# Quantised FFN weights stored untransposed and read back by transposing DMAs, in place of 132 TensorE transposes

## The chip, the cores and the metric

One Trainium2 chip, one of its cores. The metric is the time of one execution on the device in microseconds (us), median over runs. The core has TensorE (PE, with a separate row PEld for its weight loads), VectorE (DVE), ScalarE (ACT), GpSimd (POOL) and SyncE (SP). In this kernel SP issues almost every DMA, and its queue is worked through in order.

## The reference, cut to what matters

The input is `x` of 8 x 512 rows of 512 numbers, with a context of 8 x 77 rows of 384. One layer is a cross attention (8 heads of 64) and a feed-forward block whose weights and activations are fake-quantised to 8 bit.

```python
def _act_fake_quant(x, clip_factor):
    scale = sigmoid(clip_factor) * max(abs(x)) / 127       # one scale for the whole tensor
    return clip(round(x / scale), -128, 127) * scale
def _weight_fake_quant(w):
    scale = max(abs(w), axis=1, keepdims=True) / 127       # one scale for each row
    return clip(round(w / scale), -128, 127) * scale

x = x + xattn(layernorm(x), ctx, Wq, Wk, Wv, Wo, bo)
xq = _act_fake_quant(layernorm(x), clip_x)
gate, up = xq @ wq(w_gate).T, xq @ wq(w_up).T              # w_gate, w_up: 1408 x 512
h = _act_fake_quant(silu(gate) * up, clip_down)
x = x + h @ wq(w_down).T                                   # w_down: 512 x 1408
```

The two activation scales are maxima over everything, so the block falls into three stages that can't overlap on TensorE: attention for all rows, gate and up for all rows, down for all rows. The weights are contracted over their last dimension, so TensorE needs them with that dimension on the partitions: transposed.

## The kernel before

Work is cut into 8 batches `b` of 512 rows and 32 tiles `n` of 128 rows. Every instruction of every engine is put into a queue in program order by `Chain.add` (L18) and `Chain.dma` (L34, whose issue is recorded as L37), with the semaphore waits written out by hand. An engine takes its queue in order, and so does SP.

The attention stage is the loop `attend(s)` over s = 0 to 31, with b = s // 4 and t = s % 4. Step s makes the scores of tile s+1 (`S`, `soft_*`), the probabilities' transposes of tile s (`PT`, L425), the output projection of tile s-5 (`wo`, L459 to 461), its residual sum `x1` (`residual`, L485) and its second norm `n2` for tile s-6 (`normed`, L509). `x1` and `n2` go to HBM (`x_rows`, `n_rows`) from rings of three buffers: `residual(n)` waits for the store of `x1` of tile n-3, `normed(n)` for the store of `n2` of tile n-3. The query product `q_chunk` for the batches ahead needs `xTs`, the input split in two parts by `split_hi` (ACT, L208) and `split_lo` (POOL and DVE, L212); those stand in steps t = 2 and t = 3, and the first `q_chunk(b + 2, 0)` (L846) at the end of step t = 3. At the end of step t = 0, after the last product of `PV(b - 1, 3)`, SP issues `load_vb(b)` (L357), twelve small DMAs, and `load_kb(b + 1)`.

Beside it the FFN weights are quantised, one row block `i` per step, 26 in all: 22 of gate and up (128 x 512) and 4 of down (128 x 1408, `big` below). Step s issues `w_load(s)` on SP (L681), takes the row maximum, scale and inverse of block s-1 on DVE (L552 to L561), rounds it on ACT (L568) and makes the integers `wint` on POOL (`w_integer`, L574). One step later `w_turn` (L588) transposes `wint` on TensorE, 4 times 128 x 128 for a small block and 11 times for a big one, `w_out` (L597) evicts PSUM to `wstg` on ACT, and SP stores it to the scratch `wgud` or `wdd` in runs of 128 numbers. The scratch is laid out as the later stages want it in SBUF.

At the end of step 31 SP loads the whole of `wgud` into `wgu` (2816 KB, L885) with a plain DMA. It waits for `gone`, the last readers of the SBUF that `wgu` takes over. After the loop come the last tiles: `wo(27)`, `normed(26)`, `residual(27)` (L891), the products `PV(7, 0)` to `PV(7, 3)`, whose ACT and DVE evictions stand behind those two in their queues, then `wo(28)` to `wo(31)`. The first FFN product waits for `wgu` and the quantised activations. `wd` (1408 KB, L949) is loaded after the first scale is known, and needed in the last stage.

Of the kernel before, what the change touches and what calls it, by code (L numbers as in the profile page):

```python
# [5 lines left out]
class Chain:  # L6
# [27 lines left out]
    def dma(self, engine, out, in_, waits, sig):  # L34
        f32, f32r = mybir.dt.float32, mybir.dt.float32r
        out, in_ = (v.bitcast(f32) if v.dtype == f32r else v for v in (out, in_))
        return self.add(engine, lambda e: e.dma_start(out, in_), waits, sig, 16)  # L37

    def run(self, engine, e):
        for need, fn, sem, by in self.queue[engine]:  # L40
# [14 lines left out]
def block_kernel(nc, x, xT, ctxT, Wq, Wk, Wv, Wo, bo, clip_x, clip_h, w_gate, w_up, w_down, out):  # L55
    f32, f32r, bf16 = mybir.dt.float32, mybir.dt.float32r, mybir.dt.bfloat16
    ALU, ACT, AX = mybir.AluOpType, mybir.ActivationFunctionType, mybir.AxisListType
    NB, L, H, D, I = 8, 77, 8, 512, 1408
    NT, NI = 32, 11
    HL = H * L  # L60
    MAGIC = 12582912.0
# [4 lines left out]
    with ctx:  # L66
        c = Chain(nc, ctx)
        add, dma = c.add, c.dma

        def sb(stack, name, shape, dt=f32):  # L70
            return stack.enter_context(nc.sbuf_tensor(name, shape, dt))

        def dram(name, shape, dt):
            return nc.dram_tensor(name, shape, dt, kind="Internal").ap()
# [2 lines left out]
        vd = dram("v_halves", (NB * L, 2, D), f32)  # L77
        x1d = dram("x1_rows", (NT, 128, D), f32)
        n2d = dram("n2_rows", (NT, 128, D), f32)
        wgud = dram("wgu_ints", (128, 4, 2 * I), bf16)  # L80
        wdd = dram("wd_ints", (128, NI, D), bf16)
        hd = dram("h_spill", (2, 128, NI * 512), f32)


# [65 lines left out]
        vbd = sb(late, "vbd", [128, 2, 8, 128], f32r)  # L150
        pts = sb(late, "pts", [128, 2, 5, 512], f32r)
        wraw = sb(late, "wraw", [128, 2, I])
        wint = sb(late, "wint", [128, I], bf16)
        wstg = sb(late, "wstg", [128, 2, NI, 128], bf16)
        late.close()
        early.close()

# [372 lines left out]
        wg_v = w_gate.rearrange("(r p) n -> r p n", p=128)  # L530
        wu_v = w_up.rearrange("(r p) n -> r p n", p=128)
        wd_v = w_down.rearrange("(r p) n -> r p n", p=128)
        t_wr, t_wy, t_wb, t_wt, t_we, t_ws, t_wiv = [Tokens() for _ in range(7)]
        t_we["last"] = None


        W_ORDER = [*range(22)]
# [3 lines left out]
        def w_row(i):  # L541
            i = W_ORDER[i]
            return (wg_v[i], 4) if i < 11 else (wu_v[i - 11], 4) if i < 22 else (wd_v[i - 22], NI)
# [27 lines left out]
        def w_integer(i):  # L571
            n = w_row(i)[1]
            v = wraw[:, i % 2, 0:n * 128]
            t_wb[i] = add("pool", lambda e: e.tensor_scalar(wint[:, 0:n * 128], v, -MAGIC, 1.0, ALU.add,  # L574
                                                            ALU.mult), [t_wy[i], t_wt.get(i - 1)], "w_int")

        MIb = MI[:, :].bitcast(bf16)

        PTb = PTP[:, :].bitcast(bf16)

        def w_turn(i, n):

            nb = w_row(i)[1]
            dst = [(MIb if k < 8 else PTb)[:, (k if k < 8 else k + 2) * 128:][:, 0:128] for k in range(nb)]

            def fn(e):
                for k in range(nb):
                    m = e.transpose(dst[k], wint[:, k * 128:k * 128 + 128], identB[:, :])  # L588
                return m
            t_wt[i] = add("pe", fn, [t_wb[i], t_idB, t_we.get("last")] + ([t_pl[n - 1]] if nb > 8 else []),  # L590
                          "w_tr")

        def w_out(i, n, part):
            nb = w_row(i)[1]
            src, k0, k1, t = ((MIb[:, 0:1024], 0, min(nb, 8), None),
                              (PTb[:, 1280:1664], 8, nb, t_PT.get(n) if nb > 8 else None))[part]
            t_we["last"] = add("act", lambda e: e.activation(  # L597
                wstg[:, i % 2, k0:k1, :], src[:, 0:(k1 - k0) * 128].rearrange("p (k c) -> p k c", c=128),
                ACT.Copy), [t_wt[i], t, t_ws.get(i - 2)], "w_ev")
            if part == 1:  # L600
                return
            at = W_ORDER[i]
            out_ = wgud[:, :, at * 128:at * 128 + 128] if at < 22 else wdd[:, :, (at - 22) * 128:(at - 21) * 128]
            t_ws[i] = dma("sp", out_, wstg[:, i % 2, 0:nb, :], [t_we["last"]], f"st_w{i % 2}")


        for k in range(3):
            t = copy("act", wvs[:, 0, k, :], wvr[:, k, :], [t_wv], "wv_hi")
# [44 lines left out]
        def attend(s):  # L653

            b, t = s // 4, s % 4
            on = {"s": s + 1 < NT, "x": s + 3 < NT, "wo": s >= 5, "n2": s >= 6, "am": s >= 7, "w": 1 <= s < 27,
                  "turn": 2 <= s < 28, "pv": t == 0 and b >= 1}

            big = on["turn"] and w_row(s - 2)[1] > 8

            def when(key, fn, *args):
                if on[key]:
# [5 lines left out]

            def turned():

                if big:
                    w_turn(s - 2, s)
                PT(s)
                if big:
                    w_out(s - 2, s, 1)
                PT_high(s)
                if big:
                    w_out(s - 2, s, 0)

            if s < 26 and s != 2:  # L680
                w_load(s)  # L681
# [3 lines left out]
            if t == 0:  # L685
# [18 lines left out]
                when("pv", PV, b - 1, 2)  # L704
                if s > 0:
                    soft_exp(s + 1)
                if big:
                    w_turn(s - 2, s)
                PT(s)
                when("am", largest, s - 7)  # L710
                when("s", soft_sum, s + 1)
# [3 lines left out]
                    load_vb(b)  # L715
                if 1 <= b and b + 1 < NB:
                    load_kb(b + 1)
                if big:
                    w_out(s - 2, s, 1)
                PT_high(s)  # L720
                if big:
                    w_out(s - 2, s, 0)
                if t not in DEFER:
                    PT_low(s)
                when("w", w_round, s - 1)
# [96 lines left out]
                    first_bias(n)  # L822
            when("s", soft_norm, s + 1)
            more = t == 2 and b + 2 < NB
            if on["turn"] and not big:
                w_turn(s - 2, s)
                w_out(s - 2, s, 0)
            if more:
                for k in range(2 if s == 2 else 3):
                    split_lo(b + 2, k)  # L830
# [27 lines left out]
        t_dgs = []  # L858

        def spread_scale():  # L860

            def fn(e):
                for r in range(4):
                    m = e.matmul(MI[:, r * 128:r * 128 + 128], ones[:, :],
                                 wraw[:, 0, r * 128:r * 128 + 128], start=True, stop=True)
                return m
            t = add("pe", fn, [*t_dgs, t_we["last"]], "sd_mm")
            t_dgs.append(copy("dve", sdb[:, :], MI[:, :], [t], "sdb"))

        for s in range(32):  # L870
            attend(s)
            if s == 1:
                t_flat = [t_v[4], t_v[3], t_wol, ("qo_mm", c.count["qo_mm"])]
                load_vb(0)
            if s == 28:

                for r in range(4):
                    dgt = wraw[:, 0, r * 128:r * 128 + 128]
                    t = add("dve", lambda e, r=r, dgt=dgt: e.tensor_scalar_mul(
                        dgt, identF[:, :], wsc[:, 22 + r:23 + r]),  # L880
                        [t_idF, t_wsc[25], t_wb[24], t_wb[25]], "dg")
                t_dgs.append(t)
            if s == 31:
                gone = [t_S[31], t_qlo[7], t_ws[24], t_ws[25]]
                t_wgu = dma("sp", wgu[:, :], wgud.rearrange("p k n -> p (k n)"), gone, "ld_wgu")  # L885

        t_sdb = t_dgs[-1]

# [57 lines left out]
        t_g1 = whole_scale(0, amx[:, :], [("amx", c.count["amx"])])  # L946

        flown = [t_x1s[n] for n in range(28, 32)] + [t_n2s[n] for n in range(28, 32)]
        t_wdl = dma("sp", wd[:, :, :], wdd, flown + [t_g1, t_sdb, t_ws[24], t_ws[25]], "ld_wd")  # L949
        PB = PTP[:, :].bitcast(bf16)  # L950
        t_q1, t_q2, t_qt, t_nT, t_g, t_u, t_sil, t_h, t_hm = [Tokens() for _ in range(9)]

# [245 lines left out]
```

How the kernel before makes its waits and increments, by code:

```python
    def run(self, engine, e):  # L39
        for need, fn, sem, by in self.queue[engine]:
            for s, v in need:
                e.wait_ge(s, v)
            ins = fn(e)
            if sem is not None:
                ins.then_inc(sem, by)
```

## Time and profile before

| | |
|---|---|
| median of 3 runs | 619.23 us (618.63 to 621.66) |
| span of the profiled execution | 618.3 us |
| PE busy | 580.7 us (94%) |
| DVE / ACT / POOL busy | 514.6 (83%) / 331.1 (54%) / 259.9 (42%) us |
| attention stage | 0 to about 351 us |
| gate and up | 358.5 to about 516 us |
| down | about 522 to 618 us |

In a row of the lines or timeline views an operation is written `out<-in` by the program's names, followed by shape, count, and in brackets the idle time before it and what ended that. `QO`, `SP`, `PTP`, `WOP` and `MI` are PSUM tensors. `SPq` is a DMA issue on SP.

### The profile page before, as it was taken

What the parts mean: (1) busy time and instruction counts of PE and PEld (TensorE: products, weight loads), DVE (VectorE), ACT (ScalarE), POOL (GpSimd) and SP (SyncE); (2) the same over time, 40 slices, a digit from 0 to 9 for tenths busy, and PEclk for the clock granted to TensorE, in tenths of its full rate; (3) what the DMA queues carried; (4) which work ended last, traced back from release to release, by engine and by line L of the source; (5) the groups of instructions that cost most, each with busy time, mean ns of one, the idle gap of its engine ahead of it and who ended that gap; (6) DMA issues with size and microseconds to landing.
All of it is one profiled execution on the core that took longest, in us unless ns stands there. A gap on an engine that the chain in (4) does not pass through costs nothing.

```text
span 618.3 us, 8954 instructions
## 1 busy us (share of the span) xinstructions
PE 580.7 (94%) x3071; PEld 392.9 (64%) x3071; DVE 514.6 (83%) x913; ACT 331.1 (54%) x474; POOL 259.9 (42%) x321
## 2 busy tenths in 40 slices
PE   5999799999999999999999999999999999889896
PEld 2887678887888878788777844444444446334342
DVE  3867896978979799796996678899888988889994
ACT  3933455466564566544443466666666645993210
POOL 7556846757566585664632200000000000366664
PEclk9999899999999999999999999999999999979999
DMA  8979255747568464745427754370210010198974
GB/s 313 332 275 309 86 163 168 250 119 217 180 200 264 141 196 135 222 131 156 143 81 278 263 191 188 138 248 7 68 69 2 23 46 1 58 296 296 314 260 170
DMA packets 70717, 108.15 MB, mean 175 GB/s; under 512 B 32169, under 2 KB 32169, under 8 KB 70161
## 3 DMA queue, kind: packets, MB, share of 16 engines
q1 hardware_dynamic: 70669, 107.59, 52.9%
q8 instruction: 24, 0.39, 0.2%
q14 instruction: 20, 0.16, 0.1%
q10 hardware_dynamic: 4, 0.00, 0.0%
HBM read 64.75 MB, written 42.83 MB: 174 GB/s over the span
## 4 chain that ended last, share of the span: by engine, by line
PE 47%; issue 13%; SPq 10%; DVE 9%; DMA 9%; POOL 5%; ACT 5%; DVEq 0%; POOLq 0%; ACTq 0%
SPq L37 10%; PE QO L1000 10%; PE SP L1000 10%; PE QO L184 5%; PE QO L186 4%; PE QO L185 4%; POOL n2b L1118 4%; DMA wraw<-in_ffn_w_up 2%; PE WOP L459 2%; PE WOP L460 2%; PE WOP L461 2%; DMA out<-n2b 2%; DMA wraw<-in_ffn_w_gate 2%; ACT xTs L208 1%; DMA ctr<-in_ctxT 1%
## 5 line engine op out<-in xcount | busy, mean ns | idle before, releaser
L1118 POOL TENSOR_TENSOR n2b<-n2b 128x512 f32<-128x512 f32 x31 | 54.0, 1755 | 209.7 <-DVE n2b L1116 209.7
L1000 PE MATMUL QO<-nT,wgu 128*128 128x512 bf16 x352 | 90.3, 379 | 0.6 <-ACT nT L208 0.6
L1000 PE MATMUL SP<-nT,wgu 128*128 128x512 bf16 x352 | 90.3, 379 | 0.0
L1006 ACT ACTIVATE sil<-QO,fsc 128x512 f32<-128x512 f32 x88 | 60.5, 687 | 50.7 <-PE QO L1000 45.1
L1010 DVE SCALAR_TENSOR_TENSOR h<-SP,fsc,sil 128x512 f32<-128x512 f32 x88 | 65.9, 749 | 14.9 <-PE SP L1000 14.9
L418 POOL TENSOR_TENSOR P<-P,rs 128x616 f32<-128x616 f32 x32 | 39.0, 1220 | 80.8 <-DVE rs L412 80.8
L1074 ACT ACTIVATE h<-h,magic,g 128x1536 f32<-128x1536 f32 (+2 forms) x38 | 48.6, 1355 | 29.4 <-DMA h<-h_spill 25.6
L1013 DVE TENSOR_REDUCE hmx<-h 128x1 f32<-128x512 f32 x88 | 60.4, 686 | 3.0
L1000 PEld LDWEIGHTS SP<-nT,wgu 128*128 128x128 bf16 x352 | 34.4, 98 | 41.5
L184 PE MATMUL QO<-xTs,wqs 128*128 128x512 f32 x128 | 51.9, 406 | 5.7 <-POOL xTs L212 2.7
L1000 PEld LDWEIGHTS QO<-nT,wgu 128*128 128x128 bf16 x352 | 33.2, 98 | 35.4 <-ACT nT L208 0.7
L186 PE MATMUL QO<-xTs,wqs 128*128 128x512 f32 x128 | 50.8, 397 | 0.0
L185 PE MATMUL QO<-xTs,wqs 128*128 128x512 f32 x128 | 50.5, 395 | 0.0
L459 PE MATMUL WOP<-wos,os 128*128 128x512 f32 x116 | 46.5, 401 | 0.2 <-DVE x L485 0.2
L568 ACT ACTIVATE wraw<-wraw,magic,wiv 128x512 f32<-128x512 f32 (+1 forms) x26 | 24.2, 930 | 41.3 <-DVE wiv L561 41.3
L460 PE MATMUL WOP<-wos,os 128*128 128x512 f32 x116 | 45.8, 395 | 0.0
L461 PE MATMUL WOP<-wos,os 128*128 128x512 f32 x116 | 45.7, 394 | 0.0
L403 ACT ACTIVATE P<-P,r 128x616 f32<-128x616 f32 x32 | 25.9, 810 | 36.8 <-DVE P L399 36.8
L552 DVE TENSOR_REDUCE wmx<-wraw 128x1 f32<-128x512 f32 (+1 forms) x26 | 21.1, 811 | 26.2 <-DMA wraw<-in_ffn_w_up 13.4
L480 POOL TENSOR_TENSOR xn<-xn,bob 128x512 f32<-128x512 f32 x32 | 41.3, 1296 | 0.0
L376 PE MATMUL SP<-kbd,qs 128*128 128x154 f32 x128 | 35.9, 280 | 5.1 <-DVE qs L200 4.8
L198 ACT ACTIVATE os<-QO 128x512 fp32r<-128x512 f32 x32 | 19.2, 599 | 36.4 <-PE QO L186 36.3
(168 smaller groups left out, 1429.6 us busy)
## 6 DMA issues: line engine op xcount, KB each, us to landing
xTr<-in_xT SPq DMA_DIRECT2D x8, 1024.0 KB, 7.2
xn<-in_x SPq DMA_DIRECT2D x32, 256.0 KB, 4.8
x_rows<-x SPq DMA_DIRECT2D x32, 256.0 KB, 3.3
n_rows<-n SPq DMA_DIRECT2D x32, 256.0 KB, 3.8
n2b<-n_rows SPq DMA_DIRECT2D x32, 256.0 KB, 4.6
n2b<-x_rows SPq DMA_DIRECT2D x32, 256.0 KB, 3.6
out<-n2b SPq DMA_DIRECT2D x32, 256.0 KB, 2.7
h_spill<-h SPq DMA_DIRECT2D x2, 2816.0 KB, 9.4
```

The source lines that it names most:

```text
L37: return self.add(engine, lambda e: e.dma_start(out, in_), waits, sig, 16)
L184: e.matmul(ps, lh, rh, start=(i == 0), stop=False)
L185: e.matmul(ps, lh, rl, start=False, stop=False)
L186: m = e.matmul(ps, ll, rh, start=False, stop=(i == n - 1))
L459: e.matmul(wo_bank(n), os_[:, 0, j, w], wos[:, 0, j, :], start=(j == 0), stop=False)
L460: e.matmul(wo_bank(n), os_[:, 0, j, w], wos[:, 1, j, :], start=False, stop=False)
L461: return e.matmul(wo_bank(n), os_[:, 1, j, w], wos[:, 0, j, :], start=False, stop=(j == 3))
L1000: m = e.matmul(ps, wv_[:, k, col:col + 128], nT[:, b % 2, k, :], start=(k == 0), stop=(k == 3))
L1006: t_sil[n] = add("act", lambda e: e.activation(sil[:, n % SR, :], gp, ACT.Silu, scale=fsc[:, ic:ic + 1]), [t_g[n], t_fs, t_h.get(n - SR)] ...
L1010: t_h[n] = add("dve", lambda e: e.scalar_tensor_tensor(out=hv, in0=up, scalar=fsc[:, 11 + ic:12 + ic], in1=sil[:, n % SR, :], op0=ALU.mult ...
L1013: t_hm[n] = add("dve", lambda e: e.tensor_reduce(hmx[:, n:n + 1], hv, AX.X, ALU.max, apply_absolute_value=True), [t_h[n]], "hmx")
L1118: t_oa[m] = add("pool" if m < NT - 1 else "dve", lambda e: e.tensor_tensor(xo[:, so, :], xo[:, so, :], xo[:, m % 4, :], ALU.add), [t_om[m] ...
```

## The change

The scratch tensors hold the integers as they come, one row of weights in one row of the scratch: `wgud` is (2816, 512) and `wdd` (512, 1408). `wint` gets a second buffer, and its store, in runs of a whole row, is issued by `w_integer` itself. `w_turn`, `w_out` and `wstg` are gone: 132 TensorE transposes in 26 groups and 30 ACT evictions. The reads of `wgud` and `wdd` become transposing DMAs, each one instruction on SP. That of `wgu` moves from the end of step 31 to the end of step 28, since only `wqs` and the `xTs` buffers lie under `wgu`, and it now waits for the last query product and the last two weight stores alone. The transposing read of `wd` stays where the plain one was. `n2b`, loaded later in the same queue, keeps its waits.

```diff
+    def dma_turn(self, out, in_, waits, sig):
+        return self.add("sp", lambda e: e.dma_start_transpose(out, in_), waits, sig, 16)
...
-        wgud = dram("wgu_ints", (128, 4, 2 * I), bf16)
-        wdd = dram("wd_ints", (128, NI, D), bf16)
+        wgud = dram("wgu_ints", (2 * I, D), bf16)
+        wdd = dram("wd_ints", (D, I), bf16)
...
-        wint = sb(late, "wint", [128, I], bf16)
-        wstg = sb(late, "wstg", [128, 2, NI, 128], bf16)
+        wint = sb(late, "wint", [128, 2, I], bf16)
...
         def w_integer(i):
...
-            t_wb[i] = add("pool", lambda e: e.tensor_scalar(wint[:, 0:n * 128], v, -MAGIC, 1.0, ALU.add,
-                                                            ALU.mult), [t_wy[i], t_wt.get(i - 1)], "w_int")
...
+            t_wb[i] = add("pool", lambda e: e.tensor_scalar(wint[:, i % 2, 0:n * 128], v, -MAGIC, 1.0, ALU.add,
+                                                            ALU.mult), [t_wy[i], t_ws.get(i - 2)], "w_int")
+            r = W_ORDER[i]
+            out_ = wgud[r * 128:r * 128 + 128, :] if r < 22 else wdd[(r - 22) * 128:(r - 21) * 128, :]
+            t_ws[i] = dma("sp", out_, wint[:, i % 2, 0:n * 128], [t_wb[i]], f"st_w{i % 2}")
...
-            if on["turn"] and not big:
-                w_turn(s - 2, s)
-                w_out(s - 2, s, 0)
...
+            if s == 28:
+                t_wgu = c.dma_turn(wgu[:, :].rearrange("p (k n) -> p k n", k=4), wgud,
+                                   [t_qh[7, 3], t_ws[24], t_ws[25]], "ld_wgu")
             if s == 31:
-                gone = [t_S[31], t_qlo[7], t_ws[24], t_ws[25]]
-                t_wgu = dma("sp", wgu[:, :], wgud.rearrange("p k n -> p (k n)"), gone, "ld_wgu")
+                gone = [t_S[31], t_qlo[7]]
...
-        t_wdl = dma("sp", wd[:, :, :], wdd, flown + [t_g1, t_sdb, t_ws[24], t_ws[25]], "ld_wd")
+        t_wdl = c.dma_turn(wd[:, :, :], wdd, flown + [t_g1, t_sdb, t_ws[24], t_ws[25]], "ld_wd")
```

## Rows read from the trace of the kernel before

**Rows 1.** Table by stretch: length, busy PE, PEld, DVE, ACT, POOL, clock, DMA share, GB/s.

```profile
161.78:199.73 37.95, 37.19 (x215) 31.08 (x212) 32.57 (x67) 21.61 (x34) 24.20 (x35) 1.00 0.63 194
```

**Rows 2.** Waits of DVE: for what, us in total, times, longest.

```profile
DVE wmx L552 <- DMA wraw<-in_ffn_w_up: 13.4, 3, 4.8
DVE wmx L552 <- DMA wraw<-in_ffn_w_gate: 12.8, 3, 4.4
```

**Rows 3.** SP's queue in time, 161 to 174 us: start, length, issue.

```profile
161.78 9.90 SPq L37 DMA_DIRECT2D vbd<-v_halves  x12
...
172.28 0.42 SPq L37 DMA_DIRECT2D n_rows<-n  x1
172.75 0.63 SPq L37 DMA_DIRECT2D wgu_ints<-wstg  x1
```

**Rows 4.** Chain of waits in time, 173 to 187 us: start, length, what.

```profile
173.42 4.71 DMA wraw<-in_ffn_w_gate
...
182.75 0.38 ACT wstg L597
...
185.28 1.03 DVE xTs L212
```

**Rows 5.** Timeline of PE, 185 to 200 us.

```profile
185.84 0.39 PE L588 MATMUL MI<-identB,wint 128*128 128x128 bf16 x4
186.45 0.47 PE L184 MATMUL QO<-xTs,wqs 128*128 128x512 f32 x1 [0.23 <-DVE xTs L212]
...
199.50 0.40 PE L588 MATMUL MI<-identB,wint 128*128 128x128 bf16 x4
199.70 0.32 PE L376 MATMUL SP<-kbd,qs 128*128 128x154 f32 x1
```

**Rows 6.** Timeline of PE around the last group of weight transposes.

```profile
300.41 0.39 PE L588 MATMUL MI<-identB,wint 128*128 128x128 bf16 x4
300.81 0.50 PE L459 MATMUL WOP<-wos,os 128*128 128x512 f32 x1
```

**Rows 7.** Groups by form: the ACT evictions that go.

```profile
L597 ACT ACTIVATE wstg<-MI 128x512 bf16<-128x512 bf16 x22 | 12.8, 583 | 0.0
```

**Rows 8.** SP's queue in time, 321 to 332 us.

```profile
321.69 0.42 SPq L37 DMA_DIRECT2D x_rows<-x  x1
...
329.46 0.32 SPq L37 DMA_DIRECT2D wgu<-wgu_ints  x1
331.33 0.32 SPq L37 DMA_DIRECT2D n_rows<-n  x1
```

**Rows 9.** DMA issues at 329.46 and 331.33 us: KB each, us to landing.

```profile
wgu<-wgu_ints SPq DMA_DIRECT2D x1, 2816.0 KB, 10.5
n_rows<-n SPq DMA_DIRECT2D x1, 256.0 KB, 9.2
```

**Rows 10.** Table by stretch: two of the DMA queue.

```profile
161.80:171.70 9.90, 9.90 (x64) 8.68 (x62) 9.83 (x19) 7.33 (x11) 5.64 (x5) 1.00 0.18 47
329.40:340.00 10.60, 10.55 (x46) 8.20 (x45) 6.43 (x11) 3.92 (x6) 1.88 (x6) 1.00 0.96 341
```

**Rows 11.** Timeline of DVE, ACT and PE, 330 to 334 us.

```profile
330.31 0.69 DVE L485 TENSOR_TENSOR x<-WOP,xn 128x512 f32<-128x512 f32 x1 [1.13 <-PE WOP L461]
330.49 0.81 ACT L509 ACTIVATE n<-x,mr,r 128x512 f32<-128x512 f32 x1 [1.56 <-POOL mr L503]
...
333.08 0.50 PE L184 MATMUL QO<-pts,vbd 128*128 128x512 f32 x1
```

**Rows 12.** Table by stretch: PE idle, then its clock.

```profile
70.00:72.70 2.70, 0.10 (x1) 0.00 (x0) 2.67 (x3) 1.18 (x3) 2.62 (x3) 1.00 0.11 25
74.20:76.00 1.80, 1.80 (x5) 1.41 (x5) 0.72 (x2) 0.00 (x0) 1.80 (x3) 0.50 0.14 32
```

**Rows 13.** Timeline of SP and PE at the start of the gate stage.

```profile
356.63 2.60 SPq L37 DMA_DIRECT2D n2b<-n_rows  x4
...
358.45 1.02 PE L1000 MATMUL QO<-nT,wgu 128*128 128x512 bf16 x4 [0.56 <-ACT nT L208]
```

More of the change, by code:

```diff
@@ L532, in block_kernel @@
         wd_v = w_down.rearrange("(r p) n -> r p n", p=128)
-        t_wr, t_wy, t_wb, t_wt, t_we, t_ws, t_wiv = [Tokens() for _ in range(7)]
-        t_we["last"] = None
+        t_wr, t_wy, t_wb, t_ws, t_wiv = [Tokens() for _ in range(5)]
         W_ORDER = [*range(22)]
@@ L573, in w_integer @@
             v = wraw[:, i % 2, 0:n * 128]
-            t_wb[i] = add("pool", lambda e: e.tensor_scalar(wint[:, 0:n * 128], v, -MAGIC, 1.0, ALU.add,
-                                                            ALU.mult), [t_wy[i], t_wt.get(i - 1)], "w_int")
[L577 to L604, printed above, removed]
+            t_wb[i] = add("pool", lambda e: e.tensor_scalar(wint[:, i % 2, 0:n * 128], v, -MAGIC, 1.0, ALU.add,
[3 more added lines that the diff above has]
+            t_ws[i] = dma("sp", out_, wint[:, i % 2, 0:n * 128], [t_wb[i]], f"st_w{i % 2}")
         for k in range(3):
@@ L656, in attend @@
             on = {"s": s + 1 < NT, "x": s + 3 < NT, "wo": s >= 5, "n2": s >= 6, "am": s >= 7, "w": 1 <= s < 27,
-                  "turn": 2 <= s < 28, "pv": t == 0 and b >= 1}
-            big = on["turn"] and w_row(s - 2)[1] > 8
+                  "pv": t == 0 and b >= 1}
             def when(key, fn, *args):
@@ L669, in turned @@
             def turned():
-                if big:
-                    w_turn(s - 2, s)
                 PT(s)
-                if big:
-                    w_out(s - 2, s, 1)
                 PT_high(s)
-                if big:
-                    w_out(s - 2, s, 0)
             if s < 26 and s != 2:
@@ L706, in attend @@
                     soft_exp(s + 1)
-                if big:
-                    w_turn(s - 2, s)
                 PT(s)
@@ L717, in attend @@
                     load_kb(b + 1)
-                if big:
-                    w_out(s - 2, s, 1)
                 PT_high(s)
-                if big:
-                    w_out(s - 2, s, 0)
                 if t not in DEFER:
@@ L824, in attend @@
             more = t == 2 and b + 2 < NB
-            if on["turn"] and not big:
-                w_turn(s - 2, s)
-                w_out(s - 2, s, 0)
             if more:
@@ L866, in fn @@
                 return m
-            t = add("pe", fn, [*t_dgs, t_we["last"]], "sd_mm")
+            t = add("pe", fn, t_dgs, "sd_mm")
             t_dgs.append(copy("dve", sdb[:, :], MI[:, :], [t], "sdb"))
```

## The prediction, made before the changed kernel had run

> **What bounds the kernel now.** I read the page's busy row first: PE is busy 94% of the span, so the removal of PE work looks like time saved at its full length. The table by stretch asks whether that holds where the weight transposes stand, which is in the attention stage only, from 66 to 301 us. The loop has a period of one batch, four steps; the stretch of 37.95 us [rows 1] is one of them, from one `load_vb` to the next. PE is busy in 37.19 us of it at full clock, DVE in 32.57. So PE has 0.8 us to spare, and DVE 5.4.
>
> The spare time of DVE is one hole. The view of waits shows DVE waiting for a raw weight block six times for 26.2 us, 4.2 to 4.8 us each [rows 2]. Why that load is late stands in SP's queue: when PE has finished the last product of `PV`, SP issues the twelve small DMAs of `load_vb`, which take it 9.9 us, then the load of keys, a store of `n2` (0.42), the store of a transposed weight block (0.63), and only then the raw weight load of step t = 1 [rows 3]. The load takes 4.71 us to land, DVE then takes maximum, scale and inverse, ACT rounds and splits the input, DVE splits its part by 186.31, and PE starts the query product at 186.45 [rows 4].
>
> The timeline of PE closes the loop. The query product has waited 0.23 us for that split [rows 5], although PE was the engine with nothing to spare. From 186.45 to the end of `PV` at 199.50 PE works without a gap and without one weight transpose; the next group stands at 199.50, behind the product that releases `load_vb` [rows 5]. So the period is a ring: `load_vb` to the query product, 24.7 us through SP, DMA, DVE and ACT, then 13.1 us of PE. PE's transposes lie in the part of PE's time that runs beside the first piece. PE and this ring end within a quarter of a microsecond of each other, and whatever is taken from PE alone turns into a longer wait at 186.45.
>
> **The change part by part.** All terms are made against the profiled execution: span 618.3 us, 0.9 below the median of 619.2.
>
> *The TensorE transposes.* A small group delays the next instruction by 0.20 us (199.50 to 199.70) [rows 5], so 132 transposes are worth 132 x 0.05 = 6.6 us if PE alone were the bound. By the ring they are worth nothing in the six batches in which DVE waits for the load. The last group, at 300.41, stands after the last such load; the next instruction starts 0.40 later [rows 6]. That I count: 0.4 us. Bounds for this term: 0.4 and 6.6.
>
> *The evictions on ACT.* 22 of 0.58 us [rows 7] and four pairs of big ones. ACT is busy in 21.61 of 37.95 us [rows 1], so its time is spare. One eviction stands on the ring in the batches with a big block: 0.38 us at 182.75 [rows 4]. DVE, however, works through its queue from the landing to the split without a hole, and would only just use it. I take 0; the other end is 4 x 0.38 = 1.5 us.
>
> *The stores.* The weight store moves from behind `w_out` to behind `w_integer`, to one block later in number but the same place in SP's queue. It waits for the integers of block i; the `w_load` behind it in the queue waits for the same instruction already, because it reuses that raw buffer. So no new wait arises on SP, and nothing behind it (stores of `x1` and `n2`, the input load) is later by more than the issue. POOL's new wait, for the store of two blocks earlier, ends long before, and its old wait for PE goes. What does change is the store's form. In one run per row it should cost SP about what the store of `n2` costs, 0.42 against 0.63 [rows 3], and be less in the way of the load that lands after it: its 128 KB move in runs of 256 bytes now, at a full rate of 47 / 0.18 = 261 GB/s if I read that from the stretch that holds only such runs, against 341 / 0.96 = 355 GB/s in large runs [rows 10], 0.50 us against 0.37. Together 0.3 us on the ring, six times: 2.0 us. Bounds 0 and, with the evictions, 3.5.
>
> Gain in the attention loop: 0.4 + 2.0 = 2.4 us, bounds 0.4 and 8.6.
>
> *The read of `wgu`.* It was issued at 329.46, after the last store of step 31, and took 10.5 us [rows 8, 9]; nobody waited for it, since the first gate product starts at 358.45, released by the activations [rows 13]. Now it stands at the end of step 28, in SP's queue just ahead of the store of `x1` of tile 24 at 321.69 [rows 8]. Behind it are that store, then that of `n2` of tile 23. What happens to a store behind the big read is on record: `n2` issued at 331.33 took 9.2 us and landed at 340.53, 0.57 after the read's 339.96 [rows 8, 9]. The queue is served in order. So with T for the transposing read from issue to landing, the two stores land at 321.7 + T + 0.6 and + 1.1.
>
> Before, nobody needed the delayed stores for 9 us. The two that would be delayed now are needed soon: `residual(27)` writes the buffer of `x1` 24, and started at 330.31; `normed(26)` writes that of `n2` 23, and started at 330.49 [rows 11]. Each is at the head of an in-order queue, and behind them stand the evictions of `PV(7, 0)`, without which the third product of `PV` finds no PSUM bank; it started at 333.08, hardly after the bank came free [rows 11]. With 0.4 us that ACT had to spare there, PE comes late by (321.7 + T + 1.1) - 330.5 - 0.4 = T - 8.1, and from there to the gate stage the chain is PE and the latencies of the last tile, so the delay stays.
>
> T has no row. The floor is the plain read of the same bytes, 10.5 us. The far end is the stretch in which DMAs of 256-byte runs are issued one by one, 47 GB/s [rows 10]: 2.88 MB would take 61 us. I take a value near the floor, since it is one issue and not hundreds: a transpose of blocks 128 wide reads runs of 256 bytes, and at 261 GB/s in place of 341 [rows 10] the 10.5 us become 13.7. The delay is then 13.7 - 8.1 = 5.6 us.
>
> The Trainium skill ("DMA: Bandwidth & Descriptors", section Latency and other measured facts) gives a transposing DMA 261 GB/s where the middle dimension is not contiguous and 350 to 400 GB/s otherwise; no run so far shows either. By the lower of these T would be an estimated 11 us and its landing, and the sum hardly other than mine.
>
> *The clock.* With PE idle for nearly all of 2.7 us, the granted clock went from 1.00 to 0.50, 1.2 GHz, for at least 1.8 us after it resumed [rows 12]. A wait of 5.6 us before the third `PV` product should bring the same: 0.9 us lost. Bounds 0 and twice that.
>
> *The read of `wd`.* Issued where it was. Behind it in the queue is the `n2b` load for batch 2 [rows 13], which is needed one batch of gate and up after 358.45, some 19 us later. It hides up to some 18 us; half the bytes of `wgu` take less unless T is above 35. Cost 0.
>
> Sum: -2.4 + 5.6 + 0.9 = +4.1 us. 618.3 + 4.1 + 0.9 = 623.3 us.
>
> **The rivals.**
>
> *Cheap transposing read, not slower.* If T is that of a plain read, 10.5 us, PE comes late by 2.4 us, too short an idle time for the clock to fall in [rows 12], and this cancels the 2.4 us gained: 618.3 + 0.9 = 619.2 us. The sum passes +3.1 us, 0.5%, at T = 12.7: below it, this case; above it, the forecast. For it: 341 GB/s was reached by a plain read [rows 10], and one instruction issues it all. Against: a transpose must write in short pieces. The Trainium skill ("Advanced Engine Details and Errata", section X-Bar Transpose (TRN2)) says that transpose DMAs are as fast as regular ones, which is this case exactly.
>
> *PE was the bound after all, faster.* If the ring has slack that a wait of 0.23 us hides, for instance because DVE's tasks rearrange, the 6.6 us count in full, and with T = 10.5 the sum is -6.6 + 2.4 = -4.2: 615.0 us. With T = 13.7 it comes to 0. For it: PE is busy in 37.19 of 37.95 us [rows 1]. Against: PE waits at the one place where the ring meets it [rows 5], and DVE waits 4 us at another [rows 2].
>
> *A slow transposing read.* T = 30, about three times the plain one: late by 21.9, clock 0.9, sum +20.4, 639.6 us. The gate stage itself would wait only from T above 36, so the whole cost comes through the two stores.
>
> *It is no single fast stream.* If the reads are broken up as the `load_vb` ones are, T = 61, PE late by 52.9, and the time 670 us.
>
> **How the numbers follow.** Forecast case, T from 12.7 to 20: 0.36, all slower. Cheap read: 0.26, same. PE the bound: 0.20, of it 0.16 faster and 0.04 same. Slow read: 0.12. Broken up: 0.06. Slower by over 0.5% thus 0.54, within it 0.30, faster 0.16; 0.5% is about what a measurement can tell from no change here. The range goes from 615.0, the case in which PE counts, to 640.0, the slow read; outside lie the broken-up read and what is beyond 615.0. The predicted time is that of the forecast case, 623.3 us.
>
> **What would show it.** In the profile after: no L588 and L597; periods of the batches from `load_vb` to `load_vb` of 37.5 to 37.8 us in place of 37.95, with PE's wait for `xTs` at the query product up from 0.23 to over 1 us; DVE's wait for the weight load still at about 4 us, six times. The transposing issue at about 319, and its landing T later; `residual(27)` with a wait for a DMA of `x_rows`, `normed(26)` with one for `n_rows`, PE idle for 5 to 6 us before the third `PV(7)` product, and a granted clock of 0.5 after that. Gate, up and down as before. I am wrong if the periods shrink to 36.7 us (PE was the bound), if no store waits behind the read (the queue is not in order for it), or if T is far from 13.7, in which case the time follows T one to one.

## The result, and the profile after

The changed kernel takes 624.24 us (median of 6 runs, 621.70 and up) against 618.88 us for the kernel before: ratio 1.0072, 95% interval 1.0046 to 1.0099. It is slower by 5.4 us. One of its six runs, 632.46 us, was in a slower state of the chip and is not in the ratio. The profiled execution has a span of 622.4 us, 4.1 more than that of before.

Where the 4.1 us lie can be read from four marks. `load_vb(0)` starts 0.54 us later than before (67.42 against 66.88), `load_vb(7)` 1.90 us earlier (309.41 against 311.31), the first gate product 5.69 us later (364.14 against 358.45 [rows 13]), the last instruction 4.1 later. So the loop gained 2.4 us from its own start, the stretch behind it lost 7.6, and 1.6 came back at the end. Those 1.6 are hardly of the change: the down stage of the profiled execution of before lasts 100.3 us at a mean clock of 0.96 (518.0 to 618.3), that of after 98.9 us at 0.99 (523.5 to 622.4), and in the experiments below the mean clock of this stage lies between 0.96 and 1.00 in kernels with and without the change.

The loop after, one batch in the table by stretch (length, busy PE, PEld, DVE, ACT, POOL, clock, DMA share, GB/s), to be held against [rows 1], and DVE's waits, against [rows 2]:

```profile
162.15:199.38 37.23, 35.63 (x190) 29.98 (x190) 32.22 (x66) 18.88 (x29) 24.31 (x35) 1.00 0.61 200
```

```profile
DVE wmx L554 <- DMA wraw<-in_ffn_w_up: 13.9, 3, 5.0
DVE wmx L554 <- DMA wraw<-in_ffn_w_gate: 13.2, 3, 5.0
```

PE is busy 1.56 us less per batch, and 0.72 of that has come off the batch; the rest is idle time. DVE's hole for the late weight load is as large as before, 27.1 us in six.

The stretch behind the loop. SP's queue, against [rows 8]:

```profile
319.77 11.00 SPq L41 DMA_TRANSPOSE wgu<-wgu_ints  x1
330.82 0.57 SPq L37 DMA_DIRECT2D x_rows<-x  x1
331.44 0.43 SPq L37 DMA_DIRECT2D n_rows<-n  x1
```

The issue itself holds SP for 11.0 us. The DMA view has the read 13.1 us from issue to landing, against [rows 9]:

```profile
wgu<-wgu_ints SPq DMA_TRANSPOSE x1, 13.1
```

And the timeline of DVE, ACT and PE, against [rows 11]:

```profile
333.68 0.69 DVE L488 TENSOR_TENSOR x<-WOP,xn 128x512 f32<-128x512 f32 x1 [6.42 <-DMA x_rows<-x]
334.19 0.82 ACT L512 ACTIVATE n<-x,mr,r 128x512 f32<-128x512 f32 x1 [7.17 <-issue]
...
336.27 0.79 PE L187 MATMUL QO<-pts,vbd 128*128 128x512 f32 x1 [5.15 <-DVE os L203]
```

with the clock of that stretch in the table:

```profile
330.80:336.20 5.40, 0.32 (x2) 0.00 (x0) 2.06 (x4) 1.78 (x3) 0.00 (x0) 0.85 1.08 363
336.20:341.40 5.20, 5.13 (x12) 4.07 (x13) 1.96 (x5) 0.60 (x1) 1.01 (x3) 0.50 0.27 101
```

`residual(27)` waits 6.42 us for the store of `x1`, PE is idle for 5.15 us before the third `PV(7)` product, and then does twelve matmuls at 1.2 GHz in 5.2 us that took 2.9 before (333.08 to 335.97). Counted from `load_vb(7)`, that product starts 5.1 us later than before, and the slow clock takes 2.3 more: together 7.4 of the 7.6 us.

### The profile page after: what moved, and what is told of

Read it like the earlier page. It is cut to its first block, busy times and chain, and to the rows that moved or that the text cites. A ratio compares the mean times of both kernels' runs of the same rounds, so it can differ in the third digit from the quotient of the medians.

```text
span 622.4 us, 8588 instructions
## 1 busy us (share of the span) xinstructions
PE 569.4 (91%) x2915; PEld 387.5 (62%) x2939; DVE 513.5 (83%) x913; ACT 315.7 (51%) x444; POOL 260.0 (42%) x321
## 4 chain that ended last, share of the span: by engine, by line
PE 47%; issue 13%; DVE 11%; SPq 10%; DMA 9%; POOL 6%; ACT 3%; DVEq 0%; POOLq 0%
SPq L37 10%; PE SP L960 10%; PE QO L960 10%; PE QO L187 4%; POOL n2b L1078 4%; PE QO L189 4%; PE QO L188 4%; DMA wraw<-in_ffn_w_up 2%; DMA wraw<-in_ffn_w_gate 2%; PE WOP L462 2%; PE WOP L464 2%; PE WOP L463 2%; DMA out<-n2b 2%; DVE qs L203 1%; DMA v_halves<-vst 1%
## 5 line engine op out<-in xcount | busy, mean ns | idle before, releaser
L960 PE MATMUL QO<-nT,wgu 128*128 128x512 bf16 x343 | 88.7, 379 | 1.2 <-ACT nT L211 0.8
L554 DVE TENSOR_REDUCE wmx<-wraw 128x1 f32<-128x512 f32 (+1 forms) x26 | 21.2, 814 | 27.1 <-DMA wraw<-in_ffn_w_up 13.9
```

The costliest lines, as they stand in the source:

```text
L960: m = e.matmul(ps, wv_[:, k, col:col + 128], nT[:, b % 2, k, :], start=(k == 0), stop=(k == 3))
```

## The experiments

The theory after the comparison has two parts. In the loop, a ring (a closed chain of waits, from one batch's `load_vb` to the next) through SP, the weight load, DVE and PE sets the period, so PE's transposes are worth little. Behind the loop, the early read delays two stores, and the stores hold up PE, for a wait and a spell of low clock. Rivals: the transposing read does harm by itself, wherever it stands; SP's 11.0 us issue is what delays the stores, and not the order of the DMA queue; PE is the bound of the loop.

Each experiment was timed beside the kernel before, and its ratio is to that kernel's runs on the same chip.

**The read at its old place.** The changed kernel with:

```diff
-            if s == 28:
-                t_wgu = c.dma_turn(wgu[:, :].rearrange("p (k n) -> p k n", k=4), wgud,
-                                   [t_qh[7, 3], t_ws[24], t_ws[25]], "ld_wgu")
             if s == 31:
                 gone = [t_S[31], t_qlo[7]]
+                t_wgu = c.dma_turn(wgu[:, :].rearrange("p (k n) -> p k n", k=4), wgud,
+                                   gone + [t_ws[24], t_ws[25]], "ld_wgu")
```

> The changed kernel with one thing put back: the transposing read of wgu stands at the end of step 31, where the plain read stood, and waits for what that one waited for. Theory (the two stores behind the read hold PE up): the read is issued at about 327.5 us, the stores behind it are not needed before about 343 us, PE has no wait before the third PV(7) product and its clock stays at 1.00 there. What is left is the gain of the loop alone, about 1.9 us by the two traces: 616.5 to 617.5 us against 618.9 before. Rival (a transposing read slows other work wherever it stands, by sharing DMA engines or SBUF ports): still 622 us or more. Second rival: the read is now late for the gate stage, which would show as a wait of PE for a DMA of wgu at about 356 us.

Measured: 618.81 us (616.05 to 620.51), before 619.12, ratio 0.9987 (0.9962 to 1.0012). The long wait for `x_rows` and PE's wait behind it are gone, and the gate stage starts at 358.67. The read takes 14.0 us to land and nobody waits for it. So the loss of the change lies in the read's place. The transposing read isn't quite free here either: a late `residual` waits 0.92 us for a store of `x1` (344.10), and the stretch from `load_vb(7)` to the gate stage is 48.12 us, 1.0 more than before; that the one makes the other is not shown. The expected gain of the loop, 616.5 to 617.5 us, was missed. The profiled execution shows one of its batches at 39.07 us, and inside it this:

```profile
182.00:184.00 2.00, 2.00 (x9) 1.93 (x10) 1.46 (x5) 2.00 (x4) 2.00 (x3) 0.50 0.64 223
```

```profile
181.25 0.34 PE L379 MATMUL SP<-kbd,qs 128*128 128x154 f32 x1 [1.96 <-DVE qs L203]
```

PE was idle for 1.96 us, and after it the granted clock was at 1.2 GHz for about 3 us: its mean is 0.93 in the 2 us before these and 0.72 in the 2 us behind. The batch was 1.6 to 1.9 us longer than its neighbours (37.14 and 37.43). A wait for `qs` of 1.1 to 2.1 us stands in every one of the six batches once the transposes are gone, in place of 0 to 1.5 before; the clock falls after some.

**Plain reads at the new place.** The changed kernel with plain DMAs of the same bytes in place of both transposing ones (the weights come back untransposed, so the products are of other numbers):

```diff
-                t_wgu = c.dma_turn(wgu[:, :].rearrange("p (k n) -> p k n", k=4), wgud,
+                t_wgu = dma("sp", wgu[:, :], wgud.rearrange("(p r) d -> p (r d)", p=128),
...
```

> The changed kernel with both transposing reads replaced by plain reads of the same bytes, the first still at the end of step 28. The weights then come back untransposed, so the gate, up and down products are of the wrong numbers; the work is the same. Theory (order in the queue and T set the delay): T is 10.5 us, the issue takes 0.3 us, the stores land at about 331.2 us, PE late by about 2 us with no loss of clock, 618.5 to 619.5 us. Rival (the stores are late because SP itself is held by the issue of the transposing DMA for 11.0 us, and the DMA queue is not in order): with an issue of 0.3 us the stores land at once, no wait at all, 616.5 to 617.5 us.

Measured: 623.91 us (620.13 to 627.25), ratio 1.0067 (1.0031 to 1.0102). The number expected was missed: by its median this is as slow as the change. Its runs spread with their mean clock, 620.13 and 620.99 us at 0.992, 625.44 to 627.25 at 0.978 to 0.983. The trace decides between the two mechanisms. SP is free after 0.36 us and issues the store of `x1` at 319.90. DMA issues from 319.2 us on, with the time to landing:

```profile
wgu<-wgu_ints SPq DMA_DIRECT2D x1, 2816.0 KB, 12.6
...
x_rows<-x SPq DMA_DIRECT2D x1, 256.0 KB, 12.5
```

The store takes 12.5 us behind the read, though it was issued in time: it is the order in the DMA queue that holds it, and SP's long issue isn't needed for the delay. The read takes 12.6 us here, 2.1 more than the plain one of before [rows 9], with stores waiting right behind it. PE waited 4.34 us and then did seven matmuls at the low clock. From `load_vb(7)` to the gate stage it takes 53.24 us, against 54.73 in the changed kernel and 47.14 before: most of the loss there comes with a plain read too, and 1.5 us of it only with the transposing one. The profiled execution also has one batch of 39.80 us with a mean clock of 0.96.

**The transposes alone.** The kernel before, with the stores of before (runs of 256 bytes, same place in the queue) fed from the integers directly, no `w_turn`, no `w_out`; weights untransposed, as above:

```diff
-        wint = sb(late, "wint", [128, I], bf16)
-        wstg = sb(late, "wstg", [128, 2, NI, 128], bf16)
+        wint = sb(late, "wint", [128, 2, I], bf16)
...
-            t_ws[i] = dma("sp", out_, wstg[:, i % 2, 0:nb, :], [t_we["last"]], f"st_w{i % 2}")
+            t_ws[i] = dma("sp", out_, wint[:, i % 2, 0:nb * 128].rearrange("p (k c) -> p k c", c=128), [t_wb[i]],
+                          f"st_w{i % 2}")
```

> The kernel before without the 132 TensorE transposes and their evictions: the integers are stored untransposed by the same DMAs at the same place in the queue, in the same runs of 256 bytes, from two buffers of integers, and read back plain. The weights are therefore wrong; all else is as before. Ring theory: PE's time is worth nothing in the six batches, 0.4 us at the end, perhaps 1.5 us for the evictions: 617.5 to 618.7 us, batch periods of 37.8 to 38.0 us, PE's wait for xTs up to over 1 us. Rival (PE is the bound): 6.6 us less, 612.3 us, periods of 36.8 us.

Measured: 627.87 us, ratio 1.0140 (1.0113 to 1.0168). Less work, and nearly 9 us more, where 617.5 to 618.7 us had been expected. Its waits name a flaw of the experiment, here in one batch, 48.9 us in six:

```profile
POOL wint L573 <- DMA wgu_ints<-wint: 7.6, 1, 7.6
```

With the store one step behind the integers, two buffers are too few, and POOL stands for 7.6 us. The ring gets longer, PE's idle time with it, and most batches show clocks of 0.92 to 0.96 (40.54 us at 0.92 from 205.15 to 245.69). So it was run again with three buffers:

> As e3_no_turns, whose trace shows POOL waiting 7.6 us per batch for the landing of a weight store (two buffers of integers, and a store one step later than in the change): three buffers of integers in place of two, so that this wait goes. Weights wrong as there. Ring theory with the clock: the wait for xTs of PE grows to about 1.2 us per batch and the period stays at 37.8 to 38.0 us; where the granted clock falls after such a wait, a batch takes 1.5 to 2 us more. So 618 to 622 us and a mean clock of 0.98 to 0.99, no faster than before. Rival (PE is the bound and e3 was slow by the POOL wait alone): 612 to 614 us.

Measured: 618.17 us (615.50 and up), before 619.52, ratio 0.9983 (0.9957 to 1.0010). Without the transposes and evictions the kernel is not clearly faster: their 6.6 us do not come off. Its runs spread more than those of before, and they go with the mean granted clock of the execution: 615.50 us at 0.997, 616.64 at 0.996 and 0.993, 616.93 to 618.47 at 0.988, 618.79 and 620.51 at 0.985, 621.32 at 0.982, 624.25 at 0.977. The kernel before, on the same chip, has 617.79 to 619.02 us at 0.996 and 0.997. So where the clock stays up, the removal is worth something, an estimated 1 to 3.5 us by these runs, and a few falls of the clock take that back. Two neighbouring batches of its profiled execution show the price of one:

```profile
122.77:161.40 38.63, 37.13 (x191) 31.13 (x190) 32.29 (x66) 18.89 (x29) 24.33 (x35) 0.96 0.63 193
161.40:198.53 37.13, 35.63 (x190) 29.97 (x190) 32.14 (x66) 18.85 (x29) 24.33 (x35) 1.00 0.65 201
```

**The stores alone.** The kernel before with its transposes and evictions (into one buffer, and not stored), but with the stores of the change, from two buffers of integers; the reads are plain and the weights again untransposed:

```diff
+            r = W_ORDER[i]
+            out_ = wgud[r * 128:r * 128 + 128, :] if r < 22 else wdd[(r - 22) * 128:(r - 21) * 128, :]
+            t_ws[i] = dma("sp", out_, wint[:, i % 2, 0:n * 128], [t_wb[i]], f"st_w{i % 2}")
...
-            t_ws[i] = dma("sp", out_, wstg[:, i % 2, 0:nb, :], [t_we["last"]], f"st_w{i % 2}")
```

> The kernel before with the transposes and evictions kept but not stored (one eviction buffer in place of two), and the stores of the change: the integers in runs of a whole row, from two buffers, issued with the integers. Reads plain and at the old places, so the weights are wrong. Ring theory: the loop gains what the stores give, 0.3 us for each of six batches, about 2 us: 616.5 to 617.5 us, although PE does as much as before. Rival (PE is the bound): 618.9 us, no change.

Measured: 619.63 us, ratio 1.0001 (0.9979 to 1.0023). No gain, where the ring theory had expected 616.5 to 617.5 us and the rival, that PE is the bound, no change: taken alone, this number speaks for the rival, and the two experiments that follow are needed against it. The trace shows where the gain went. In one batch SP issues the weight load 11.24 us after `load_vb` instead of 11.45, but the load takes 5.4 us to land in place of 5.0. The saving on the issue was eaten by the landing; why the load lands later is not shown. Five batches take 37.4 to 38.4 us, and all six together 0.3 us less than before.

**Cutting the ring.** The weight load of step t = 1 goes out after the fourth DMA of `load_vb`, in the kernel before, with the wait for its buffer kept:

```diff
         def load_vb(b):
             at = 0
+            count = 0
             while at < HL:
+                if count == 4 and 1 <= b and 4 * b + 1 < 26:
+                    w_load(4 * b + 1, ("w_int", 4 * b))
+                count += 1
...
-            if s < 26 and s != 2:
+            if s < 26 and s != 2 and not (t == 1 and b >= 1):
                 w_load(s)
```

> The kernel before with one load moved: the raw weight load of step t = 1 is issued by SP after the fourth of the twelve DMAs of load_vb instead of behind all of them. Same work, same instructions. Ring theory: DVE's hole of 4 us goes, the query product is no longer waited for, and the period falls from 37.95 us to what PE's own work allows, 37.2 us or a little more, six times: 614.5 to 616.5 us. Rival (the ring is no bound, PE is): no change, 619 us.

Measured: 612.09 us (610.84 to 613.75), before 619.52, ratio 0.9878 (0.9853 to 0.9903). One DMA issue moved forward by 8 us is worth 7.4 us, more than the 3 to 5 expected. DVE waits for no weight block in the loop any more. The period is PE's own busy time, to the last hundredth:

```profile
160.14:196.89 36.75, 36.75 (x215) 31.06 (x212) 32.43 (x66) 21.64 (x34) 24.39 (x35) 1.00 0.65 202
```

The same edit in the changed kernel, with the read at step 31:

> The changed kernel with the transposing read of wgu put back to the end of step 31, as in e1_read31, and the raw weight load moved as in e6_early_load. Ring theory: with the ring cut, the TensorE transposes that are gone count at their full 6.6 us: period about 36.0 us, no waits of PE, so no fall of the clock: 607 to 611 us. Rival (the transposes stay worthless because another engine, DVE at 32.6 us per batch, or the softmax chain bounds the loop): the time of e6 less 2 us at most, 613 us or more.

Measured: 604.91 us (603.00 to 605.61), ratio 0.9758 (0.9734 to 0.9783), below the 607 to 611 expected.

```profile
156.51:191.77 35.26, 35.26 (x190) 29.95 (x190) 32.24 (x66) 18.80 (x29) 23.96 (x35) 1.00 0.64 211
```

Between these two kernels lies the change, its read apart, and it is worth 7.2 us: 1.5 us in each of four batches, 0.8 to 0.9 in the last two. With the ring in place it was worth nothing measurable (0.9987). This kernel beats both.

**The early read with the loop out of the way.** The same kernel with the read at step 28, which is the changed kernel plus the moved load:

> The changed kernel as it is, read of wgu at the end of step 28, with only the moved weight load of e6 and e7. Against e7_change_early31 it differs by the place of that read alone, in a kernel whose loop loses no time to the ring. Theory: 5.1 us of wait and 2.4 us of half clock, less the little that differs in the gate stage: 611.5 to 613 us against 604.9. Rival (what the changed kernel lost came mostly from the loop's clock): 606 to 608 us.

Measured: 610.98 us (610.73 to 611.68), ratio 0.9867 (0.9845 to 0.9889). The place of the read alone costs 6.1 us by the medians, a little under the 6.6 at least that were expected. PE's wait is there, 5.33 us, and the low clock after it lasted for some seven matmuls and not twelve (mean clock 0.64 from 324.8 to 329.0).

**The early read in halves.** The gate half of the rows at step 28, the up half at step 31:

```diff
+                t_wgu0 = c.dma_turn(wgu3[:, :, 0:I], wgud[0:I, :], [t_qh[7, 3], t_ws[24], t_ws[25]], "ld_wgu0")
...
+                t_wgu = c.dma_turn(wgu3[:, :, I:2 * I], wgud[I:2 * I, :], gone, "ld_wgu")
```

> The changed kernel with the moved weight load of e6 and e7, and the read of wgu cut in two halves by rows: the gate half at the end of step 28, the up half at the end of step 31. Theory (cost is T less the 8 us for which the stores behind it are not needed): each half takes 6.5 to 7.5 us, so neither holds residual(27) or normed(26) up; 604 to 606 us, as e7_change_early31. Rival (a transposing read has a large fixed cost, or any big read at that place stalls PE): 608 us or more, with a wait of DVE for x_rows.

Measured: 604.47 us (603.66 to 607.29), ratio 0.9765 (0.9740 to 0.9791), as the kernel with the whole read at step 31. SP's queue:

```profile
306.42 5.91 SPq L41 DMA_TRANSPOSE wgu<-wgu_ints  x1
316.31 6.47 SPq L41 DMA_TRANSPOSE wgu<-wgu_ints  x1
```

Half the rows take SP about half as long, 5.91 us against 11.0, so most of the issue grows with the amount of work. The halves took 7.9 and 10.0 us to land, more than the 6.5 to 7.5 expected, and still short enough: DVE's wait for the store falls from 6.6 to 1.5 us and PE's from 5.33 to 0.35.

**Keeping the clock.** Matmuls on ones, put on PE in the changed kernel in front of the third `PV(7)` product, to fill its wait:

```diff
         PV(7, 1)
+
+        def warm_mm(e):
+            for _ in range(45):
+                m = e.matmul(MI[:, 0:128], ones[:, :], ones[:, :], start=True, stop=True)
+            return m
+        add("pe", warm_mm, [t_sdb])
         PV(7, 2)
```

> The changed kernel with 45 matmuls of 128 columns on ones, to an unused PSUM bank, put on PE between the second and the third PV(7) product, where it waits 5.15 us for the eviction behind the stores. They fill about that wait. Theory: the wait stays as long, but the granted clock stays at 1.00 after it, so the 2.4 us go that the twelve matmuls at half clock cost there: 621.5 to 622.5 us against 624.2. Rival (the clock falls anyway, or its fall costs nothing): no change or later, 624 us or more.

Measured: 626.70 us, ratio 1.0120 (1.0089 to 1.0151), not faster than the change and far from the 621.5 to 622.5 expected. I had sized them wrongly: one such matmul on 4-byte numbers is two entries, 90 in 10.2 us, twice the wait. Again with 23:

> As e8_warm_tail with 23 matmuls in place of 45: there each took two entries of 0.113 us, 10.2 us in all, twice the wait of 5.15 us they should fill. Now about 5.2 us. Theory: the third PV(7) product starts when it does in the changed kernel, the clock stays at 1.00, and the stretch of twelve PV matmuls takes 2.8 us in place of 5.2: 621.5 to 622.5 us against 624.2. Rival: the loss of clock is made good elsewhere, 624 us.

Measured: 625.56 us (623.17 and up), ratio 1.0119 (1.0082 to 1.0155): not faster than the change, and the 621.5 to 622.5 us expected were missed again. The clock was kept, 1.00 from 334 us on, and the `PV(7)` matmuls went at full speed:

```profile
330.88 5.30 PE L860 MATMUL MI<-ones 128*128 128x128 f32 x46
337.55 0.50 PE L187 MATMUL QO<-pts,vbd 128*128 128x512 f32 x1 [1.37 <-DVE os L203]
```

But in the profiled execution the store of `x1`, issued at 330.82 in both, took 3.9 us to land in place of 2.7 (`residual(27)` waited 7.7 us and not 6.4), so PE resumed at 337.55 instead of 336.27. The stretch from `load_vb(7)` to the gate stage is still 0.9 us shorter than in the profile of the change (53.87 against 54.73), but the medians show no gain. That the fill keeps the clock is shown; that it saves time is not.

## Why the prediction was right, point by point

**The forecast**, 623.3 us and slower, stands against 624.24. The sum for the profiled execution was +4.1 us and the span grew by 4.1. That is luck as far as it is this close: the stretch behind the loop lost 7.6 us where 6.5 were forecast, 1.6 came back through the clock of the down stage, which no term foresaw, and the loop started 0.5 later. The medians are 5.4 apart. What was right is the direction and the largest term, the delay by the stores.

**The ring, right.** PE's transposes were counted at 0.4 of 6.6 us because PE already waited for `xTs` and DVE for the weight load. Removing them and their evictions alone changed nothing measurable (0.9983), and with the ring cut the whole change but the read's place was worth 7.2 us, slightly more than the 6.6. But 0.4 was too little for an execution whose clock stays up, as the runs above show.

**PE's wait, right in kind and wrong in place.** I expected it to grow to over 1 us at the query product. It appeared earlier, at the scores, which need DVE's part of `qs`, and DVE makes that right behind the late weight maximum. The trace of before shows that wait already, and I had not read it: in the batch of [rows 1] PE waits 0.53 us for `qs` at 181.05, more than the 0.23 us for `xTs`. PE in the changed kernel, one batch later than [rows 3 to 5]:

```profile
218.96 0.34 PE L379 MATMUL SP<-kbd,qs 128*128 128x154 f32 x1 [2.07 <-DVE qs L203]
...
223.80 0.47 PE L187 MATMUL QO<-xTs,wqs 128*128 128x512 f32 x1
```

From 218.96 to the query product at 223.80 PE has work without a gap and no transposes in it, and the last `xTs` is ready before. The ring now runs over `qs`, not over `xTs`.

**The stores and the evictions, right in sum by luck and wrong in cause.** The loop was to gain 2.4 us, of it 2.0 from the stores and none from the evictions, with falls of the clock not thought of. It gained 2.4 us in the profiled execution from its own start, but as two parts: the six batches from `load_vb(1)` to `load_vb(7)` are 3.4 us shorter, and the first, from `load_vb(0)` to `load_vb(1)`, is 1.0 us longer. The clock goes with that 1.0: first before, then after.

```profile
66.88:86.27 19.39, 14.97 (x79) 11.91 (x79) 15.74 (x28) 9.43 (x17) 12.89 (x15) 0.91 0.37 100
67.42:87.82 20.40, 15.73 (x73) 12.52 (x74) 15.70 (x27) 7.84 (x14) 12.82 (x15) 0.83 0.33 102
```

PE waits 2.7 us in this batch in both; after it the clock is at 0.50 until some 77 us before, and until past 78 after. The profiled executions of all the kernels here fall into these two groups, 19.3 to 19.7 us at 0.91 and 20.3 to 20.5 us at 0.83, with and without the change.

And the stores alone gave nothing measurable. In the batch that starts at 199.38 us DVE's weight maximum starts 16.69 us after `load_vb`, against 16.45 before: no gain up to there. The gain lies behind it, where DVE ends its `xTs` at 223.65, 7.6 us after that maximum started, against 8.1 before (216.18 to 224.32), once neither eviction nor weight transposes stand between. The run without the transposes, which keeps the stores of before, bears this out: its four batches at full clock are 0.2 to 0.8 us shorter than before. So the term that was mis-sized is the evictions and the transposes on the ring, taken at 0 with 1.5 as the bound for the evictions, and the store term was mostly nothing.

**The delay by the stores, right.** T, the time of the read from issue to landing, was put at 13.7 us and measured 13.1; PE was to come late by T - 8.1, 5.6 us, and waited 5.15. With the measured T the rule gives 5.0 us here, 4.5 for the plain read (T = 12.6, waited 4.34) and 5.2 in the kernel with the moved weight load (T = 13.3, waited 5.33). The reasoning that an in-order queue carries the delay from the read to the stores is confirmed by the plain read, where SP was free and the store still took 12.5 us. What I had not seen is that the issue of a transposing DMA also holds SP, 11.0 us for `wgu` and 8.1 us for `wd`; here it ended 2.1 us before the read did, and the store landed some 0.7 us behind the read, against 0.3 in the run with the plain one, so it cost a few tenths at most. The read of `wd` cost nothing, as forecast: from the first gate product to 522 us PE is idle for 0.8 us, as in the runs that read `wd` plainly.

**The price of T, near by luck.** Its rate was taken from the stretch of 256-byte runs, 261 GB/s. In the after's trace of the read's stretch, 319.8 to 332.9 us, the DMA view has:

```profile
DMA packets 11722, 3.43 MB, mean 262 GB/s; under 512 B 11477, under 2 KB 11477, under 8 KB 11721
```

2816 rows of four runs of 256 bytes are 11264 packets: the read moves in the pieces that were assumed. The rate is not shown to be the assumed one: 262 GB/s is all that moved in the stretch, and the read alone makes 2.88 MB in 13.1 us, 220 GB/s from issue to landing. Nor do the short pieces explain the step from 10.5 to 13.1 us: a plain read at the same place takes 12.6. The Trainium skill ("DMA: Bandwidth & Descriptors", section Latency and other measured facts) states 261 GB/s for a transposing DMA whose middle dimension is not contiguous. The 262 GB/s of this trace are those of all DMAs together and so no test of that figure.

**The rival of the cheap read, wrong at its base.** It took the plain read's 10.5 us as its floor. At the new place a plain read takes 12.6 us, so the floor was not to be had there, and by the medians a plain read at that place is as slow as the change (1.0067 and 1.0072). Its second premise, that a wait of 2.4 us is too short for the clock to fall, had no row either; with the read put back the clock fell after 1.96 us. The cost is in what stands behind the read. The Trainium skill ("Advanced Engine Details and Errata", section X-Bar Transpose (TRN2)) says that transpose DMAs are as fast as regular ones. At the new place the two differ by 0.5 us, 13.1 against 12.6, but at the old one by 3.5, 14.0 against 10.5, and there the measurement speaks against the rule.

**The clock, mis-sized.** 0.9 us was the part of a spell that my row covered; the spell lasted for all twelve `PV(7)` matmuls, 5.2 us for 2.9, so 2.3 us. And the larger miss is that the clock wasn't considered in the loop, where PE's new wait of 1.1 to 2.1 us per batch lets it fall in some batches, for 1.5 to 2 us each. In the profile of the change with its read put back (618.8 us by the median, where the loop alone promised 617) one such batch and the slower first one cost about 1.8 and 1.0 us; how many there are in the other runs is only to be guessed from their mean clocks.

**Still open:** why the low clock of the first batch lasts longer in some profiled executions than in others; why a plain read of the same bytes takes 2.1 us more at the early place than at the late one; and why the store landed later in the run with the filling matmuls.

## What to carry to other kernels

An engine that is busy 98% of a period can still be worth next to nothing: look for the one short wait in it and for the hole on another engine, and follow the ring between them before removing work. Here one DMA issue, moved 8 us forward in its queue, ahead of eight of the twelve small loads, was worth 7.4 us, and made the change without its early read worth 7.2 more; together 604.9 us against 619. A large DMA should be placed by who needs the stores behind it in the same queue, not by when its own data are wanted, and a wait that is left on TensorE can cost a second time through its clock.

## What the runs showed of the hardware

- A transposing DMA from HBM is one instruction on SP, but its issue holds the queue: 11.0 us for 2816 x 512 (10.5 to 11.4 in the other runs), 5.9 and 6.5 us for halves of the rows, 8.1 us for 512 x 1408, half the bytes (6.2 to 8.2 in the other runs). It moves in pieces of under 512 bytes and took 13.1 us for 2.88 MB at step 28 and 14.0 at step 31, against 12.6 and 10.5 for plain reads there.
- A 256 KB store issued right behind a 2816 KB read took 12.5 us to land, against 2.3 us for one issued at 326.75 us in the kernel before, with no large DMA ahead of it.
- TensorE's granted clock went to 0.50 after idle times of 1.96 and 5.15 us, and stayed at 1.00 after one of 2.07 us. With 23 filling matmuls it stayed at 1.00.
